# Second layer's target rows of chunks 0 and 1 by broadcasting DMAs, with the gate, the combine and the attention placed anew among chunk 3's experts

## What is computed

```python
def _L0_ffn_ref(x, Wg, bg, W1, b1, W2, b2):          # first mixture: 8 experts, top 2
    gate_scores = jnp.einsum('bsd,ed->bse', x, Wg) + bg
    topk_scores, topk_idx = jax.lax.top_k(gate_scores, K)
    topk_probs = jax.nn.softmax(topk_scores, axis=-1)
    combine = jnp.sum(topk_probs[..., None] * jax.nn.one_hot(topk_idx, E, dtype=x.dtype), axis=-2)
    for e in range(E):
        h = jax.nn.relu(jnp.einsum('bsd,hd->bsh', x, W1[e]) + b1[e])
        y = jnp.einsum('bsh,dh->bsd', h, W2[e]) + b2[e]
        out = out + combine[..., e:e + 1] * y

def _L1_gnn_ref(x, adj, W, a):                        # second attention layer: 4 heads
    Whh = (x @ W.T).reshape(N, H, d_k)
    s1 = jnp.einsum('nhd,d->nh', Whh, a[:d_k, 0])
    s2 = jnp.einsum('nhd,d->nh', Whh, a[d_k:, 0])
    z = s1[:, None, :] + s2[None, :, :]
    e = jnp.where(z > 0, z, 0.2 * z).mean(-1)
    attn = jax.nn.softmax(jnp.where(adj > 0, e, -9e15), axis=1)
    return jnp.einsum('ij,jhd->ihd', attn, Whh).reshape(N, H * d_k)

x = x + _L0_gnn_ref(_layernorm(x), adj, ...)
x = x + _L0_ffn_ref(_layernorm(x)[None], ...)[0]
x = x + _L1_gnn_ref(_layernorm(x), adj, ...)
x = x + _L1_ffn_ref(_layernorm(x)[None], ...)[0]      # second mixture: routed by blocks of 32 tokens
```

## Time and profile before

| what | value |
|---|---|
| median of 3 runs | 657.49 us |
| profiled execution | 657.6 us, its span 655.8 us |
| TensorE matmul busy | 553.6 us, 84% of the span |
| VectorE busy | 512.8 us, 78% |
| ScalarE busy | 375.4 us, 57% |
| GpSimd busy | 177.0 us, 27% |
| DMA moved | 76.25 MB, 116 GB/s in the mean |
| mean granted TensorE clock | 0.936 |

### The profile page before, as it was taken

How to read it: one execution, slowest core, us unless ns; L and a number is a source line. 1 busy time by engine, 2 the same in 40 slices (tenths; PEclk the granted TensorE clock), 3 DMA queues, 4 the chain that set the end, 5 groups by cost and what they waited for, 6 DMA issues and landing times.

```text
span 655.8 us, 13298 instructions
## 1 busy us (share of the span) xinstructions
PE 553.6 (84%) x5094; PEld 431.5 (66%) x5094; DVE 512.8 (78%) x904; ACT 375.4 (57%) x762; POOL 177.0 (27%) x186
## 2 busy tenths in 40 slices
PE   1979783999999999799998799789999546999985
PEld 1668682788775877767686494468778446566743
DVE  6499979995697857799848755998998998999420
ACT  1698692668876777586755836552422101566563
POOL 4211133031102100984522010030223000364741
PEclk9979995989998999899998999889999877799999
DMA  6477740022065156999597120020204744375650
GB/s 143 85 136 141 208 99 0 18 78 67 21 208 193 45 182 209 197 212 236 115 208 90 54 66 0 1 65 0 65 1 133 240 114 127 115 208 178 206 168 17
DMA packets 48265, 76.25 MB, mean 116 GB/s; under 512 B 5334, under 2 KB 24798, under 8 KB 48202
## 3 DMA queue, kind: packets, MB, share of 16 engines
q1 hardware_dynamic: 30122, 49.91, 24.3%
q0 software_dynamic: 15488, 22.02, 19.8%
q10 hardware_dynamic: 2592, 3.48, 2.1%
HBM read 78.51 MB, written 22.04 MB: 153 GB/s over the span
## 4 chain that ended last, share of the span: by engine, by line
PE 59%; DVE 16%; ACT 14%; issue 4%; DMA 2%; POOL 1%; SPq 1%; ACTq 1%; DVEq 0%
PE bank L675 12%; PE bank L687 10%; PE bank L604 10%; DVE arena L1586 7%; PE bank L830 5%; ACT arena L1110 5%; PE bank L876 4%; PE bank L775 4%; PE bank L867 3%; PE bank L791 2%; ACT ysb L1058 2%; PE bank L589 2%; ACT maskT L975 2%; DVE arena L1414 2%; DMA routed_sums<-in_wsT 1%
## 5 line engine op out<-in xcount | busy, mean ns | idle before, releaser
L474 POOL TENSOR_TENSOR x<-x,ysb 128x512 f32<-128x512 f32 x36 | 77.9, 2163 | 247.3 <-ACT ysb L1058 247.1
L1110 ACT ACTIVATE arena<-heads,nd 128x512 bf16<-128x512 f32 x176 | 112.1, 726 | 22.7 <-PE bank L604 22.7
L675 PE MATMUL bank<-hTc,arena 128*128 128x512 f32 x192 | 93.0, 639 | 5.6 <-ACT reg_c L1047 5.6
L1586 DVE SCALAR_TENSOR_TENSOR arena<-reg_b,nd,arena 128x1536 f32<-128x1536 f32 x48 | 91.2, 1961 | 0.0
L687 PEld LDWEIGHTS bank<-arena,reg_c 128*128 128x128 f32 x768 | 87.6, 192 | 3.9 <-issue 3.8
L687 PE MATMUL bank<-arena,reg_c 128*128 128x128 f32 x768 | 88.4, 275 | 0.0
L604 PE MATMUL bank<-reg_b,arena 128*128 128x99 bf16 x1536 | 76.1, 213 | 3.7 <-DVE arena L1447 3.7
L604 PEld LDWEIGHTS bank<-reg_b,arena 128*128 128x128 bf16 x1536 | 75.0, 101 | 5.9 <-DVE arena L1447 3.9
L1047 ACT ACTIVATE reg_c<-bank,b 128x512 f32<-128x512 f32 x96 | 65.0, 687 | 23.2 <-PE bank L675 23.2
L1058 ACT ACTIVATE ysb<-bank,comb 128x128 f32<-128x128 f32 x128 | 36.5, 367 | 67.0 <-PE bank L876 41.3
L1433 DVE TENSOR_TENSOR arena<-maskT,arena 128x2048 bf16<-128x2048 bf16 x36 | 48.6, 1350 | 31.9 <-ACT arena L1110 31.9
(11 more groups left out here) (189 smaller groups left out, 850.6 us busy)
## 6 DMA issues: line engine op xcount, KB each, us to landing
maskT<-routed_sums SPq DMA_DIRECT2D x48, 256.0 KB, 3.1
reg_c<-in_adj POOLq DMA_DIRECT2D x16, 512.0 KB, 7.8
arena<-in_w1T SPq DMA_DIRECT2D x16, 512.0 KB, 4.0
arena<-in_w2T SPq DMA_DIRECT2D x16, 512.0 KB, 5.0
routed_sums<-in_wsT SPq DMA_DIRECT2D x32, 256.0 KB, 5.6
routed_sums<-in_wrT POOLq DMA_DIRECT2D x32, 256.0 KB, 12.2
arena<-routed_sums SPq DMA_DIRECT2D x32, 256.0 KB, 3.0
routed_sums<-ident POOLq DMA_DIRECT2D x4, 1024.0 KB, 12.3
```

The lines of the kernel that those rows point to most:

```text
L474: nc.gpsimd.tensor_tensor(xi, xi, ysb[:, e % 3, :].rearrange("p (t d) -> p t d", d=P), ALU.add).then_inc(s_acc, 1)
L675: mm(bank[b][:, :], w1[:, s, e % 2, c * P:(c + 1) * P], hTc[:, :], start=True, stop=True).then_inc(full[b], 1)
L1110: last = af(ind[:, q, b, j, :], sbc[:, h, :], ACT.Relu, bias=nd[:, q * QT + j, h:h + 1], scale=BIG)
L1586: last = v.scalar_tensor_tensor(p, row, nd[:, t, h:h + 1], p if h else maskT[:, t, columns], ALU.max, ALU.mult)
```

## The change

Rows of chunks 0 and 1 are no longer made in all partitions by TensorE. New functions `row_scores(c, b)` on TensorE and ScalarE make the four heads' scores of a chunk in four partitions (one matmul with 4 output rows, `wxs[1][:, P:P+H]` as weight) and exponentiate them there, with bias `nmx_col` (one value per partition, made by three small steps in `score_bounds`), into rows 0 to 3 (chunk 0) and 32 to 35 (chunk 1) of `hTc`. Chunk 0's stands ahead of expert pair 3's second layer for chunk 2, chunk 1's behind it. SP stores both in a DRAM buffer, waits, and then issues four transfers, one per head, that read a row of 4 KB and write it in all 128 partitions of `rows1`. Heads 0 to 2 wait until the attention of head 2 is done, head 3 until that of head 3. For this `u` is laid out by heads ((h t b) in place of (t h b)), so that a head's values cover just what the head's row overwrites, and `rows1` has a stride of a quarter of `reg_b`. Chunk 2's rows are made as before.

VectorE waits per head for its broadcast row. `gate` stands one head earlier, and the norm of chunk 3 stands behind head 2 of pair 5 in place of behind pair 4. On TensorE the third first layer stands ahead of the combine, attention 2 and 3 one expert layer or more earlier. On ScalarE the gate's exponential stands behind two experts' first layers, and the transposes and scores of chunk 3 stand behind exponents and scaled values, with a wait for the two stores (they read `hTc`).

```diff
-        u6 = u.rearrange("p (t h b) s v -> p t h b s v", t=T, h=H)
+        u6 = u.rearrange("p (h t b) s v -> p t h b s v", t=T, h=H)
-        rows1 = reg_b[:, 0:H * WW].rearrange("p (h i) -> p h i", h=H)
+        rows1 = reg_b[:, :].rearrange("p (h i) -> p h i", h=H)[:, :, 0:WW]
...
                     load_pair(c, h, c < C - 1 or h < 2)
+                    if c == C - 1 and h == 1:
+                        for r in range(2):
+                            sp.wait_ge(ev["score"], C + r)
+                            sp.dma_start(rows_l1[:, bass.ts(r, CW)],
+                                         hTc[r * GRP:r * GRP + H, :]).then_inc(s_spill, 16)
+                        sp.wait_ge(s_spill, 16 * (C + 1))
+                        for g in range(H):
+                            sp.wait_ge(full[1], C * H - 1 if g < H - 1 else C * H)
+                            sp.dma_start(rows1[:, g, 0:2 * CW],
+                                         rows_l1[g:g + 1, :].to_broadcast([P, 2 * CW])).then_inc(s_row[g], 16)
...
+            def row_scores(c, b):
+
+                pe.wait_ge(ev["hTc"], 2 * C + c)
+                use(b, "score")
+                mm(bank[b][0:H, :], wxs[1][:, P:P + H], hT[:, bass.ts(c, CW)], start=True,
+                   stop=True).then_inc(full[b], 1)
...
+                        row_scores(0, 7)
                     second_layer(h)
+                    if h == H - 1:
+                        row_scores(1, 6)
...
             project(1, 0, (5, 7))
             project(1, 1, (5, 7))
-            source_rows1(0)
-            source_rows1(1)
             ln_transpose(6, xn)
...
+            def row_scores(c, b):
+
+                act.wait_ge(s_nmx, 1)
+                got(b)
+                af(hTc[c * GRP:c * GRP + H, :], bank[b][0:H, :], ACT.Exp, bias=nmx_col[c * GRP:c * GRP + H, :],
+                   scale=SLOPE).then_inc(ev["score"], 1)
...
             source_rows1(2)
-            scores()
             exponents(1)
             scale_values(0)
+            act.wait_ge(s_spill, 16 * (C + 1))
+            scores()
             first(0)
+            first(1)
             gate()
             exponents(2)
-            first(1)
             second_layer(0, 4)
...
                 for h in heads:
+                    if g == 0:
+                        dve.wait_ge(s_row[h], 16 * C)
                     products(h, (2 * g, 2 * g + 1), wide, rows1[:, h, :], slice(0, WW), s_wide)
...
-            dve.wait_ge(ev["rows"], H + 3 * H)
+            dve.wait_ge(ev["rows"], 2 * H)
             wide_pair(0, range(2))
             best(C - 1, 2 * C - 1)
-            wide_pair(0, range(2, H))
+            wide_pair(0, range(2, 3))
             gate(C - 1, 2 * C - 1)
+            wide_pair(0, range(3, H))
             for g in range(1, 5):
                 wide_pair(g)
+            wide_pair(5, range(H - 1))
             dve.wait_ge(s_acc, C * (E0 + 1))
             norm(C - 1, 2 * C + 2)
-            for g in range(5, T // 2):
+            wide_pair(5, range(H - 1, H))
+            for g in range(6, T // 2):
                 wide_pair(g)
```

30 lines of the change are left out of this document (19 added, 11 removed).

## The result

The changed kernel took **647.09 us** (median of 4 runs, 645.76 to 650.16), the kernel before 656.74 us in the same job (655.37 to 658.99): ratio 0.984, 95% interval 0.981 to 0.987. The prediction, 644.8 us with a range of 641.0 to 650.5, was 2.3 us too low: it had forecast a gain of 12.7 us, and the medians of this job moved by 9.65. The profiled execution took 647.73 us (span 646.0).

The account below looks back on a forecast made before the run. VectorE was taken to bound the stretch from 406.47 to 542.96 us, with TensorE's expert phase stopping it three times. 657.6 - 5.8 (start) - 7.9 (stalls) + 1.0 (add) = 644.9, as median 644.8 us; range 641.0 to 650.5.

Parts of the forecast that it names:

- The start: VectorE's wide products would start at 400.7 us instead of 406.47: -5.8 us.
- The broadcasts: The four rows sent by DMA would stand between 394 and 402 us, row 0 with 6 us to spare: no cost.
- The gate: ScalarE's exponential for the gate would be done at 412.1 us, 1.8 us ahead of VectorE at 413.9.
- Rival A: TensorE's clock falls behind its wait before chunk 3's scores; VectorE waits 1.7 us at the gate: 646.5 us, chance 0.2.
- The stalls: VectorE's three stalls, two for attention's slots and one for the last expert's output, would all go: -7.9 us.
- What is late next is VectorE itself: With the stalls gone, VectorE asks for the last expert at 492.5 us, when it has been there for 2.5 us.
- The ninth add: GpSimd's add of an expert's output that fell in a stall now meets a VectorE product: +1.0 us.
- The tail: The stretch behind VectorE's end (last tiles, merge, mixture) carried over unchanged at 114.6 us.
- Rival C: VectorE's end comes earlier but the stretch behind it does not follow, 3 to 6 us stay: 650 us, chance 0.06.
- B: ScalarE's evictions break up TensorE's blocks by 1 us per expert; half the stalls return, +4: 649 us, chance 0.12.
- D: The broadcasts are slow, 15.4 us a row, and hold up VectorE by 37 us: 682 us, chance 0.03.
- E: The relayout by heads spoils or helps the first stretch: 641.8 or 648 us, chance 0.04 together.

Follow-up runs that it names:

- after_again: The changed kernel measured once more, unaltered, in another job: 647.29 us, ratio 0.986 to the kernel before.
- order_only: The kernel before with only the new order on TensorE, ScalarE and VectorE, rows still made by TensorE: 652.98 us, ratio 0.993.
- rows_only: The changed kernel's broadcast rows, small matmuls and layout by heads, with the order of before on all engines: 652.46 us, ratio 0.990.
- busy_norm: The changed kernel plus five unread matmuls in TensorE's idle time ahead of chunk 3's transposes: 648.11 us, ratio 0.986.
- y7_early: The changed kernel with the last expert's output in its own bank and chunk 3's norm one head (two products) earlier: 645.13 us, ratio 0.981.
- layout_only: The kernel before with only the values laid out by heads and the rows' wider stride: 657.7 us, ratio 1.000.
- y7_gate_busy: y7_gate plus unread matmuls at three places: ahead of chunk 3's scores, its transposes and the last wide attention: 644.48 us, ratio 0.983.
- y7_busy_all: y7_gate_busy plus three unread matmuls in TensorE's wait ahead of chunk 2's last first layer, at 370 us: 640.9 us, ratio 0.976.
- busy_last: The changed kernel plus four unread matmuls ahead of the last wide attention: 647.32 us, ratio 0.985.
- norm_back: The changed kernel with chunk 3's norm back behind pair 4, as before: 654.68 us, ratio 0.997.
- y7_gate: y7_early with the gate's exponential between the two first layers on ScalarE: 646.58 us, ratio 0.984.

## Why the prediction was right, and where it was off

The direction, the two mechanisms and the range held. The sum was 4.8 us off at VectorE's end (530.3 predicted, 535.10 measured) and 2.0 of these came back in the tail. The gain, 12.7 us in the prediction, was 9.65 in the medians.

**The start: right.** Predicted -5.8. Counted from the first layer at 370, the products start 35.50 - 30.15 = 5.35 us earlier, and 38.5 - 33.1 = 5.4 where the clock had fallen. Of the missing 0.4, the row matmuls account for 0.2 to 0.3: a run of two records took 1.02 us, not 0.86 to 0.91, and there are two. In absolute time the start was 403.44 and not 400.7: +3.0 for the slow records, -0.7 because this execution was earlier until then, +0.4 for the term.

**The broadcasts: right.** They hid. They were issued at 392.7 and not at 390, but that is again the clock at 370: from the first layer there it is 22.4 us, and in after_again, with fast records, 388.25 - 369.10 = 19.2, where the prediction had 19.0. My 2.5 us a row were too much: four rows of 512 KB stood within 7.7 us of the first issue.

**The gate: the weakest step.** I had the exponential 1.8 us ahead of VectorE, from first layers of 8 x 0.86 = 6.9 us. They took 8.81 us in the first execution and 10.13 in after_again, both behind a wait of 2.60 us; the granted clock was 0.56 from 408 to 411 in the first. In the first execution ScalarE was done at 416.6 and VectorE there at the same time. In three of the six executions with this order on ScalarE and rows in time, VectorE waited about 1.7 us. Rival A had both the mechanism and the price; its chance of 0.2 looks low against three of six. That the first profile shows no such wait is luck. The trace of before had told it: the clock had fallen behind 3.28 us.

**The stalls: right.** All three went. From the first product to pair 5 I had 81.4 us; measured 483.59 - 403.44 = 80.2. order_only and rows_only show that this is the order's doing. The last expert's add was over at 494.46, predicted 490 at the latest, and VectorE asked at 495.99; counted from the first product that is 91.0 us against 89.3, and the room 1.5 us against 2.5.

**"What is late next is VectorE itself": the step that failed.** I asked of every pair whether its slot was free, and not whether its exponents were there. Pair 6 takes chunk 3's, which need the norm, transposes, a projection and ScalarE's exponential: 507.42 - 495.74 = 11.7 us in the kernel before, where eight products (some 14 us) covered it. Behind the new place of the norm stand two, 3.6 us. Cost 2.16 us, of which 1.1 are TensorE's clock (busy_norm) and all of which goes with two products more in between and an earlier last expert (y7_early). With it gone the stretch from first product to wide end is 129.6 us, the figure that I had predicted (530.3 - 400.7), but by other parts: in y7_early VectorE waits 1.16 us for the last expert and the last two adds slow one product between them, where the prediction had 1.0 us more for the ninth add and no wait.

**The ninth add: about right.** Products beside a GpSimd add took 2.83 us again, and the add itself 1.94 in place of 1.26. In the norm, now beside GpSimd's casts, two small VectorE steps took 0.55 and 0.52 us in place of 0.16, 0.7 in sum, which I had not counted. It is a cost that moved: in the kernel before, the same casts stood beside pair 5's products, which took 3.90 and 10.80 us there in place of 3.54 and 10.46. With this, the products took 0.8 us less than predicted. The Trainium skill (GPSIMD Engine Reference, section Specifications) has the two engines share their SBUF interfaces and contend where a VectorE instruction has two SBUF inputs; the slowed steps have two, and the trace agrees, on both sides of the pair.

The ledger at VectorE's end, predicted to measured: +3.0 clock at 370, -0.7 an earlier execution, +0.4 start, +2.2 exponents, +0.7 norm, -0.8 products: +4.8. The first two terms are not the change's doing: the profile of before had fast records at 370, that of after slow ones. Without them the change falls 2.5 us short of 12.7, which fits the 9.65 of the medians.

**The tail: not carried over unchanged.** 647.73 - 535.10 = 112.6 us, not 114.6. The last wide attention took 7.19 us and not 8.55, and VectorE waited 0.87 us for its sums and not 2.23. This is not the change's doing either: among all profiled executions the tail is 111.7 to 114.6 us long, and layout_only, whose tail is that of before, has 112.6. So the 2.0 us that came back are luck of the execution. Rival C (a longer tail) is out, and so are B, D and E.

What stays open: when the fill ahead of the scores helps. The wait left there was 1.23 us in y7_gate_busy and 1.22 in y7_busy_all. In the first the 16 records behind it ran at a granted clock of 1.00, in the second they took 8.81 us as without a fill. First y7_gate_busy, then y7_busy_all:

```profile
404.67 6.25 PE L889 MATMUL bank<-hTc,arena 128*128 128x512 f32 x14
411.77 1.13 PE L889 MATMUL bank<-hTc,arena 128*128 128x512 f32 x2 [0.85 <-ACT reg_c L1256]
```

```profile
403.27 8.81 PE L894 MATMUL bank<-hTc,arena 128*128 128x512 f32 x16
```

## What to carry to other kernels

When an engine becomes the bound, list for each of its instructions all the inputs that it waits for, the small ones too, and check each against the new order: a late step that is moved (here a norm) takes its whole chain of followers with it, and what had covered them may stand on its other side now. A row of the trace behind a wait of TensorE is one draw, at a lowered clock or at full clock; look at several executions before its time goes into a sum, and count a wait of TensorE ahead of work on the path as a possible slowdown of what stands behind it. Filling such waits with matmuls that nobody reads gave the fastest kernel here, but which of the four fills earned what is not separated: one alone ahead of the transposes (busy_norm) and one alone ahead of the last attention (busy_last) did not show in a median.

## What the runs showed of the hardware

The same instructions behind the same wait of TensorE (2.82 or 2.83 us) ran at a granted clock of 1.00 in five profiled executions and at 0.50 in eight, for the same or nearly the same program ahead of them; it costs 3.0 us. Behind a wait cut to 0.25 us they ran at full clock in the one execution profiled. The last wide attention took 7.2 to 8.6 us behind waits of 2.42 to 6.84 us, in thirteen executions, and 5.60 behind one of 2.09. The length of the wait alone does not decide it: chunk 3's transposes took 1.12 us behind 3.04 us of idle time (norm_back) and 0.66 behind 3.48 and 3.65 (y7_gate, y7_early). The Trainium skill (TensorE: Matmul & The Clock Gate, section What's actually happening) takes the low clock for the default that activity releases; the trace agrees for chunk 3's projection, which was fast in all three executions with a fill ahead of it (1.20 to 1.51 us) and slow in all eight where TensorE had stood idle there (2.19 or 2.20). Where a fill left a wait of 1.2 us or more, what stood behind it was fast in two cases and slow in three.

A 4 KB row of DRAM, written to all 128 partitions, landed in 3.8 to 6.1 us, four of them in flight together: 2 MB within 7.7 us of the first issue. Behind two transfers from DRAM to DRAM on the same queue the same broadcasts landed after 16.9 to 18.9 us.
